# A per-column weight-magnitude sum moved one feed-forward half earlier in a fused attention and feed-forward layer

## What is computed

```python
def bitnet_linear(x, weight, scale_param):
    s = jnp.maximum(jnp.mean(jnp.abs(weight), axis=1), 1e-08)
    binary_w = jnp.sign(weight / s[:, None])
    y = jnp.einsum('bsi,oi->bso', x, binary_w)
    y = y * (s * scale_param)[None, None, :]
    return jnp.nan_to_num(y, nan=0.0, posinf=1000000.0, neginf=-1000000.0)

xn = _layernorm(x)
# q, k, v = bitnet_linear(xn, ...); 32 heads of softmax(q k^T / 4) v; bitnet_linear(out, o_weight, o_scale)
# ffn: (silu(xn @ gate_w.T) * (xn @ up_w.T)) @ down_w.T
x = x + attention(xn) + ffn(xn)
```

## Time and profile before

| | us |
|---|---|
| Median of 3 runs | 510.2 (509.6 to 514.09) |
| Profiled execution | 510.75 |
| Its span | 509.0 |
| TensorE busy | 485.1 (95%) |
| VectorE busy | 417.5 (82%) |
| ScalarE busy | 352.6 (69%) |
| GpSimd busy | 93.3 (18%) |
| Mean granted TensorE clock | 0.997 of full |

### The profile page before, as it was taken

The page is one execution under the profiler, slowest core; times in us unless marked ns, Lnnn a source line. Parts: engine busy times, 40 slices in busy tenths (PEclk is TensorE's granted clock), DMA queues, the critical chain, the costliest instruction groups (busy, mean ns, idle before and its releaser), DMA issues.

```text
span 509.0 us, 9735 instructions
## 1 busy us (share of the span) xinstructions
PE 485.1 (95%) x3882; PEld 161.2 (32%) x3882; DVE 417.5 (82%) x487; ACT 352.6 (69%) x655; POOL 93.3 (18%) x138
## 2 busy tenths in 40 slices
PE   1899999998999999999999999999999999999996
PEld 1564434433332222222222222222222222223442
DVE  7879769675777999999999999999999952223985
ACT  1943634342228999999999999999999987774000
POOL 4212244434323000000000000000000103241021
PEclk9999999999998999999999999999999999999999
DMA  8944773731103702102101210220210204452311
GB/s 263 278 86 100 160 146 44 204 63 21 23 0 49 139 23 62 40 24 64 40 30 56 40 57 27 42 61 23 62 41 24 62 25 121 111 151 74 105 70 55
DMA packets 31300, 38.99 MB, mean 77 GB/s; under 512 B 6608, under 2 KB 20816, under 8 KB 31256
## 3 DMA queue, kind: packets, MB, share of 16 engines
q1 hardware_dynamic: 22232, 27.34, 18.8%
q0 software_dynamic: 8304, 10.95, 11.6%
q10 hardware_dynamic: 720, 0.08, 0.1%
HBM read 33.24 MB, written 10.35 MB: 86 GB/s over the span
## 4 chain that ended last, share of the span: by engine, by line
PE 75%; ACT 15%; DVE 4%; DMA 3%; issue 2%; SPq 1%; ACTq 0%; DVEq 0%
PE ps L1219 22%; PE ps L1091 15%; PE ps L1184 13%; ACT room L674 13%; PE ps L1152 10%; PE ps L1100 7%; PE ps L1070 3%; PE ps L1245 3%; DMA room<-wo_rows 2%; ACT osb L685 1%; DMA hlo<-x 1%; PE ps L1008 1%; DVE nmx L807 1%; PE ps L1062 1%; SPq L421 1%
## 5 line engine op out<-in xcount | busy, mean ns | idle before, releaser
L807 DVE TENSOR_REDUCE nmx<-ps 128x1 f32<-128x1024 f32 x256 | 293.6, 1216 | 14.4 <-PE ps L1100 14.1
L674 ACT ACTIVATE room<-ps 128x512 f32<-128x512 f32 x512 | 274.4, 597 | 22.0 <-PE ps L1184 12.1
L1219 PE MATMUL ps<-room,vcur 128*32 128x256 f32 (+1 forms) x1912 | 160.9, 408 | 4.4 <-ACT osb L685 4.1
L1184 PE MATMUL ps<-qst,kB 50*128 50x512 f16 x512 | 149.7, 384 | 0.8 <-DVE room L906 0.5
L1100 PE MATMUL ps<-kA,qst 48*128 48x512 f16 x512 | 145.7, 383 | 2.3 <-DVE sob L880 1.8
L1091 PE MATMUL ps<-room,wf 128*128 128x512 f16 x448 | 100.7, 380 | 0.0
L1219 PEld LDWEIGHTS ps<-room,vcur 128*32 128x32 f32 x1912 | 37.7, 108 | 100.5 <-issue 53.4
L1184 PEld LDWEIGHTS ps<-qst,kB 50*128 50x128 f16 x512 | 30.7, 93 | 112.5 <-ACT room L674 102.5
L655 ACT ACTIVATE room<-ps,gsc 128x512 f32<-128x512 f32 x28 | 19.2, 685 | 60.3 <-PE ps L1091 60.3
L1091 PEld LDWEIGHTS ps<-room,wf 128*128 128x128 f16 x448 | 42.4, 98 | 54.6 <-issue 6.6
L513 POOL TENSOR_TENSOR hlo<-room,hhi 128x512 f16<-128x512 f32 x28 | 34.0, 1216 | 90.0 <-ACT hhi L585 89.9
(11 more groups left out here) (127 smaller groups left out, 267.7 us busy)
## 6 DMA issues: line engine op xcount, KB each, us to landing
qst<-q_scratch SPq DMA_DIRECT2D x32, 192.0 KB, 3.6
o_scratch<-osb SPq DMA_DIRECT2D x16, 256.0 KB, 2.3
q_scratch<-parts SPq DMA_DIRECT2D x12, 256.0 KB
hlo<-x SPq DMA_DIRECT2D x8, 256.0 KB, 4.9
parts<-x POOLq DMA_DIRECT2D x8, 256.0 KB, 4.1
wf<-gate POOLq DMA_DIRECT2D x14, 128.0 KB, 4.2
wf<-up POOLq DMA_DIRECT2D x14, 128.0 KB, 6.1
wd<-down POOLq DMA_DIRECT2D x1, 1792.0 KB, 13.3
```

Of the source, the lines that this page charges most:

```text
L674: nc.scalar.activation(probs[:, s % 2, r, :], ps[:, score_bank(entry(j, i)), :], ACT.Exp, scale=gam_reg[par][r]).then_inc(scores_free, 1)
L807: nc.vector.tensor_reduce(nmx[:, hf, idx:idx + 1], bank_pair(idx % 2), AX.X, ALU.max, negate=True).then_inc(rows_free, 1)
L1184: nc.tensor.matmul(ps[:, score_bank(e), :], kB[low:low + SROWS, par, kt % (TT // 2) * P:(kt % (TT // 2) + 1) * P], qst[low:low + SROWS, pa ...
L1219: mm = nc.tensor.matmul(ps[32 * r:32 * r + 32, 7, of], vcur[:, par, key_tile(r, j), :], probs[:, s % 2, r, of], start=(j == 0 and part == ...
```

## The change

Three steps change places in the strings, and nothing else does. TensorE takes S 1 behind A16 and ahead of F19 (it took it behind F19). VectorE takes A16's maximum and S 1 ahead of F19's product (behind it before). ScalarE takes Y 0 behind F16 and Y 1 behind F17 (behind F15 and F16 before). `SUM_AT` stays 17. Of the strings' lines, cut:

```diff
 pe_order
-... F17 A14 A15 F18 A16 F19 S1 A17 F20 T0 A18 ...
+... F17 A14 A15 F18 A16 S1 F19 A17 F20 T0 A18 ...
 dve_order
-... A12 A13 A14 F17 D1 A15 F18 F19 A16 S1 A17 F20 ...
+... A12 A13 A14 F17 D1 A15 F18 A16 S1 F19 A17 F20 ...
 act_order
-... F15 Y0 F16 Y1 F17 F18 F19 F20 T0 ...
+... F15 F16 Y0 F17 Y1 F18 F19 F20 T0 ...
```

More of the change, by code:

```diff
@@ L59, in layer_kernel @@
     pe_order = ("K0 K1 X0 X1 X2 X3 X4 X5 X6 X7 G0 P0 P1 S0 Z0 U0 Z1 G1 P2 Z2 P3 U1 F2 F3 F4 P4 P5 F5 F6 A0 F7 A1 A2 "
-                "F8 A3 A4 F9 A5 F10 F11 F12 A6 A7 F13 F14 A8 A9 F15 A10 A11 F16 A12 A13 F17 A14 A15 F18 A16 F19 "
-                "S1 A17 F20 T0 A18 A19 F21 A20 A21 F22 A22 A23 F23 A24 A25 F24 A26 A27 F25 A28 A29 F26 A30 A31 F27 ")
+                "F8 A3 A4 F9 A5 F10 F11 F12 A6 A7 F13 F14 A8 A9 F15 A10 A11 F16 A12 A13 F17 A14 A15 F18 A16 S1 F19 "
+                "A17 F20 T0 A18 A19 F21 A20 A21 F22 A22 A23 F23 A24 A25 F24 A26 A27 F25 A28 A29 F26 A30 A31 F27 ")
     dve_order = ("M0 M1 J0 M2 J1 M3 H0 M4 R0 M5 N0 N1 M6 M7 L0 H1 N2 R1 N3 N4 L1 N5 L2 N6 N7 L3 L4 L5 L6 L7 J2 S0 Z0 "
                  "g0 V0 Z1 G0 F0 Z2 g1 X0 Z3 G1 E2 F1 X1 g2 F2 G2 F3 g3 G3 X3 F4 g4 F5 G4 A0 F6 F7 A1 A2 A3 F8 A4 F9 "
[2 rows of a table removed]
[2 rows of a table added]
     act_order = ("D0 C0 C1 D1 N1 C2 N2 C3 N0 C4 B5 C5 C6 C7 B4 B2 B0 B1 B3 F0 E0 E1 F1 X0 X1 F2 E3 F3 V2 W0 X3 F4 E4 E5 "
-                 "F5 F6 X4 F7 F8 F9 F10 F11 X5 F12 F13 F14 F15 Y0 F16 Y1 F17 F18 F19 F20 T0 F21 F22 F23 F24 F25 F26 "
+                 "F5 F6 X4 F7 F8 F9 F10 F11 X5 F12 F13 F14 F15 F16 Y0 F17 Y1 F18 F19 F20 T0 F21 F22 F23 F24 F25 F26 "
                  "F27 ")
```

## The result

| | before | after |
|---|---|---|
| Median of 12 runs, us | 510.47 (509.48 to 514.52) | 508.08 (506.58 to 511.28) |
| Profiled execution, us | 510.75 | 507.6 |
| Its span, us | 509.0 | 505.9 |
| Mean granted clock, profiled execution | 0.997 | 0.999 |

The ratio of the new times to the old is 0.9943, with a 95% interval of 0.9919 to 0.9967. In a second round, ten runs beside 21 of the kernel before on one chip, it was 0.9950 (0.9932 to 0.9967), 507.39 against 510.16. So the change makes the kernel about 0.5% faster. That is within the 1% either way to which the forecast gave 0.95, and yet both intervals exclude no change.

The account below looks back on a forecast made before the run. TensorE was taken as the bound, idling only ahead of A15 and A17. Gains of 0.61 and 1.90 less 0.28 gave 2.23 us: 508.0 us against the 510.2 median (508.5 against the profiled 510.75), range 506.2 to 510.5.

Parts of the forecast that it names:

- The bound: Gate 17 to the attention loop: TensorE sets the pace, holding 75% of the chain; time gained ahead of F20 carries through.
- The second gap, 1.90: Ahead of A17: TensorE's 1.83 us idle wait for L880 goes, because S1 and L880 come sooner; 1.90 us gained.
- The first gap, 0.61: Ahead of A15: silu of 16 no longer waits for the output weights' transfer, so F18 starts 0.61 us sooner.
- the forecast of 12.68: Distance from the start of gate 17 (106.62) to A17 (119.30) in the new schedule: 12.68 us.
- The wait given back, 0.28: Ahead of S1: new wait for A15's maximum, with the weight load's 0.22 us exposed; 0.28 us lost.
- The sum: A17 at 119.30 instead of 121.53: 0.61 plus 1.90 less 0.28 gives 2.23 us, carried to the end.
- GpSimd's hold on D 1: Rival at D1: GpSimd's subtraction blocks VectorE up to 1.16 us, giving 509.1; chance 0.13, shared with a late transfer.
- The room of 0.54: At D1 on VectorE: GpSimd's subtraction was to start at 113.93, 0.54 us after D1.
- The clock: Way into the attention loop: between -1.7 and +1.7 us by the clock; the forecast took nothing.
- the dip stays away: Rival at the attention loop's start: half clock does not occur, saving up to 1.65 us, giving 506.3; chance 0.12.

Follow-up runs that it names:

- S 1 alone: Kernel before with only S1 moved ahead of F19 on TensorE, and its VectorE steps ahead of F19's product; ScalarE as before; ratio 0.9932 (0.9906 to 0.9959).
- TensorE's alone: Full change, but VectorE keeps its old order, F19's product and A16's maximum ahead of L880; ratio 1.0029 (1.0003 to 1.0054) against the kernel before.
- ScalarE's part alone: Kernel before with only ScalarE's two magnitude steps, Y0 and Y1, one gate later; ratio 0.9984 (0.9952 to 1.0015).
- the late transfer: Kernels before and after, half of `wo_rows` transferred once more ahead of the transfer; 514.61 us (ratio 1.0077) and 508.09 us (ratio 0.9941).
- the forced trace: Kernel after with GpSimd doing its subtraction of half 16 three times, to be at work across D1; one run, 513.47 us.

## Why the prediction was right, point by point

*The bound.* Right. TensorE set the pace from gate 17 to the loop, and the 2.29 us gained there stood in full at A17 and at VectorE's last product, which starts at 151.78 for 154.36: 2.58 sooner, 0.30 of them from ahead of gate 17. Behind that, the loop's last trip to memory took 0.54 in the profiled execution.

*The second gap, 1.90.* Right in cause and size. In the traces S 1 is worth 14.29 - 12.62 = 1.67 us with the new wait paid; the wait took 0.17 and S1 0.07 more, so the gap itself is 1.91. At equal clock S 1 alone is worth 1.80 +- 0.23. It needs both orders; TensorE's alone loses 1.08 us in the traces (15.37 against 14.29).

*The first gap, 0.61.* The cause is right: with a landing at 106.74 the new order has no gap ahead of A15, and with one at 108.97 the old order loses it one for one. But the term is mis-sized as a typical value: it was read from one landing. The eleven profiles of kernels with a single transfer have it at 102.8, 102.9 (twice), 103.0, 103.7, 104.1, 105.1, 106.0 (twice), 106.5 and 106.7. Only in the last four is it late enough for a gap in the old order; there the term would be 0.6 to 1.4 us, and over all eleven 0.35 on average (an estimate, from the landings, the starts of gate 17 and the 5.01 us). The runs of ScalarE's part alone give 0.47 +- 0.25. That the profile of the kernel after met the forecast of 12.68 shows S 1's part; that the difference of the two profiles met the forecast's 2.23 is in part luck, as the 0.61 stands in the same execution of the kernel before from which it was read. What the forecast gave as ScalarE's share is insurance against a late transfer: of the 2.69 +- 0.28 us that the late transfer costs the kernel before, the kernel after loses 0.10 +- 0.27.

*The wait given back, 0.28.* S1 started 0.17 us late (0.49 behind A16 for 0.32), 0.11 less than taken. The forecast added 0.05 and the load's 0.22 to the maximum's end; S1 came 0.15 behind it, and the load is 0.03 ahead of the matmul in the trace. So the load's 0.22 did not come into the open in full; why, no row shows. But S1 took 0.93 to F19's start for 0.86. With 0.01 less in each of two halves, 12.68 were forecast and 12.62 came.

*The sum.* 2.23 forecast, 2.29 in the pair of traces (1.67 of them for the landing of the kernel after), 2.39 between the medians and 2.77 in the second round, 2.07 +- 0.19 at equal clock. That the forecast of 508.0 stands 0.1 from the median of 508.08 is luck: it was taken from a median of three runs, 510.2, that twelve runs put at 510.47, and the clock's part was taken as nothing. The profiled execution was forecast at 508.5 and came at 507.6, with the dip of the clock gone.

*GpSimd's hold on D 1.* The room of 0.54 was 0.53 (the subtraction at 113.62, the maximum behind D1 at 113.09); it did not happen, and when made to happen it cost 1.88 for two meetings, 0.92 and 0.96 each, within the 1.16 at most of one. The Trainium skill's rule ("SBUF — State Buffer", section "Who interferes with whom"), of which the rows then showed no tensor_scalar, agrees with the forced trace: even the 128x4 one was kept waiting.

*The clock.* The rival "the dip stays away" came true in the profiled execution of the kernel after, and does not in every run: 9 of 22 are below 0.998. Its price was put at up to 1.65 us and is 1.12 in the pair of profiles. The forecast took nothing for the clock. For the median that was near enough, but S 1 alone shows that the clock can add as much as the schedule.

## What to carry to other kernels

When a small result passes from one engine to another and back while the first must not stand still, put a piece of the first engine's long work between the two steps, and look at the other engine's queue too: here TensorE's order alone made it 1.08 us slower, since VectorE still had another step ahead. What waits for a transfer should stand behind what does not need it, even where one trace shows the wait as short, because here the landing moved over 4 us from one profile to the next. Ask of an experiment whether the condition it is to test was there: the profile of ScalarE's part alone gave the number worked out, with an early landing for which the old order gives it too. Read a gain of half a per cent from distances inside the trace and from runs at equal clock, as the medians alone spread by as much, and then look at the clock for itself.

## What the runs showed of the hardware

- Half clock goes with most of the spread: 1.36 us around a kernel's mean become 0.68 around the fit. Each 0.001 off the mean clock goes with 0.40 us. In a span of 509 us, 0.001 of the mean is 1.02 us at half clock, so a microsecond at half clock costs about 0.4 (an estimate), less than the half I had bounded it by.
- After gaps of 0.84 and 1.83 us the profiles show TensorE at 1.00 directly behind them; with gaps of 2.69, 2.97 and 3.38 us it fell to 1.2 GHz, 0.50, behind the gap or at its very end. Two stretches of the kernel with TensorE's order alone, the first the gap itself, still at 1.00, the second from 1.9 us behind it:

```profile
119.50:122.10 2.60, 0.00 (x0) 0.00 (x0) 2.52 (x4) 0.00 (x0) 0.72 (x1) 1.00 0.00 0
...
124.00:127.50 3.50, 3.50 (x11) 1.32 (x10) 0.00 (x0) 1.19 (x2) 0.96 (x1) 0.60 0.00 0
```

The Trainium skill ("TensorE: Matmul & The Clock Gate", section "What's actually happening") has a gate that goes by how busy TensorE has been, and runs freely of the kernel's own time. That the fall comes late, and not at the same distance from each gap, agrees with it. The gap of 1.97 us forced by GpSimd was followed by 1.00 up to 155 us, where the loop opens.
- A VectorE tensor_scalar that meets a GpSimd subtraction is held until its end, and the next one can be held again by the next subtraction: 0.16 us became 1.08, and of the four behind it one was held in its turn, 1.24 us for 0.27.
- The 1 MB transfer of `wo_rows`, issued at 92.7 to 94.2 us, took 9.6 to 12.7 us in the eleven profiles of kernels with a single transfer. Its landing so falls anywhere from 102.8 to 106.7.
